# Spread rows in cleared edge records, lists and experts in one block, and a last stage shared by four engines

## What is computed

```python
xn = layernorm(x)
agg = segment_sum(xn[dst] * edge_weight[:, None], src)          # 100000 edges
gnn = relu((xn + agg) @ gW1 + gb1) @ gW2 + gb2                  # 256 -> 512 -> 256
x2  = x + gnn + (heads(xn) + xn)                                # attention without softmax, 8 heads
xn2 = layernorm(x2)
logits = xn2 @ gate_w + gate_b                                  # 16 experts
topk_vals, topk_idx = top_k(logits, 2); w = softmax(topk_vals)
y = xn2 + sum_k w_k * (relu(xn2 @ w1[e_k] + b1[e_k]) @ w2[e_k] + b2[e_k])
out = x2 + layernorm(y) * gamma + beta
```

## Time and profile before

| | |
|---|---|
| median of 3 runs | 2164.53 us (2162.41 to 2166.05) |
| profiled execution | 2162.62 us |
| its span | 2160.9 us |
| granted TensorE clock, mean | 0.884 of full |
| PE busy | 1603.4 us (74%) |
| DVE busy | 1391.8 us (64%) |
| ACT busy | 768.0 us (36%) |
| POOL busy | 1286.3 us (60%) |
| DMA | 231.99 MB, mean 107 GB/s |

### The profile page before, as it was taken

How to read it: one execution, slowest core, us unless ns; L and a number is a source line. 1 busy time by engine, 2 the same in 40 slices (tenths; PEclk the granted TensorE clock), 3 DMA queues, 4 the chain that set the end, 5 groups by cost and what they waited for, 6 DMA issues and landing times. The chain is left out here.

```text
span 2160.9 us, 38464 instructions
## 1 busy us (share of the span) xinstructions
PE 1603.4 (74%) x9490; PEld 1379.4 (64%) x9490; DVE 1391.8 (64%) x4033; ACT 768.0 (36%) x2288; POOL 1286.3 (60%) x1227
## 2 busy tenths in 40 slices
PE   6007888535777778788777877777757999999985
PEld 4006777424555666666666665665546999999964
DVE  5899888548876566666666665566434454545559
ACT  5807898400000233323333232222122333333344
POOL 0005888658877777777777777777602555555420
PEclk9657999767878999999999998999678999999999
DMA  5000110444343444444444444444834652222247
GB/s 168 0 0 20 39 37 21 21 127 137 120 122 108 128 127 129 132 128 128 128 131 132 127 128 120 127 120 128 88 68 147 198 159 71 71 72 70 68 170 278
DMA packets 132685, 231.99 MB, mean 107 GB/s; under 512 B 28678, under 2 KB 85304, under 8 KB 132391
## 3 DMA queue, kind: packets, MB, share of 16 engines
q0 software_dynamic: 56096, 144.39, 24.9%
q1 hardware_dynamic: 48727, 59.76, 9.2%
q10 hardware_dynamic: 27696, 25.83, 3.7%
HBM read 187.46 MB, written 42.43 MB: 106 GB/s over the span
## 5 line engine op out<-in xcount | busy, mean ns | idle before, releaser
L1308 POOL DMA_INDIRECT lower<-xn_rows,lower x858 | 848.0, 988 | 270.5 <-issue 234.6
L1333 PE MATMUL bank<-lower 128*128 x960 | 349.0, 449 | 211.7 <-SPq L1182 176.9
L1333 PEld LDWEIGHTS bank<-lower 128*128 128x128 f32 x960 | 175.3, 214 | 289.0 <-issue 277.7
L1471 DVE TENSOR_TENSOR xh<-xh,bank 128x256 f32 x480 | 199.5, 416 | 245.6 <-PE bank L1334 244.4
L1454 DVE TENSOR_SCALAR lower<-iota_n,lower 128x128 f32<-128x128 f32 x960 | 294.0, 359 | 76.3 <-issue 54.5
L606 POOL DMA_INDIRECT edge_records_sorted<-lower x112 | 202.6, 1809 | 209.0 <-ACT lower L755 179.1
L1334 PE MATMUL bank<-lower 128*128 x960 | 321.7, 420 | 0.0
L683 PE MATMUL bank<-lower 128*64 128x128 f32 x1568 | 190.6, 286 | 113.6 <-ACT lower L739 109.1
L683 PEld LDWEIGHTS bank<-lower 128*64 128x64 f32 x1568 | 184.5, 145 | 117.3 <-DVE lower L941 109.7
L1959 DVE TENSOR_SCALAR arena<-bank,b_tile 128x128 f32<-128x128 f32 x456 | 128.4, 344 | 165.5 <-PE bank L1893 165.5
L1893 PEld LDWEIGHTS bank<-arena 128*128 128x128 f32 x1824 | 224.6, 194 | 13.5 <-issue 7.8
(11 more groups left out here) (330 smaller groups left out, 2348.5 us busy)
## 6 DMA issues: line engine op xcount, KB each, us to landing
lower<-xn_rows,lower POOLq DMA_INDIRECT x858, 2.8
lower<-in_L_ffn_w SPq DMA_DIRECT2D x16, 512.0 KB
upper<-in_L_ffn_w SPq DMA_DIRECT2D x16, 512.0 KB
xn_rows<-xh SPq DMA_DIRECT2D x7, 896.0 KB, 4.2
lower<-xn_rows ACTq DMA_DIRECT2D x49, 128.0 KB
xn_rows<-lower ACTq DMA_DIRECT2D x49, 128.0 KB
x_plus_beta<-lower ACTq DMA_DIRECT2D x49, 128.0 KB
upper<-in_x SPq DMA_DIRECT2D x1, 6144.0 KB
```

The costliest lines, as they stand in the source:

```text
L1308: pool.indirect_dma_start(edge_rows[:, t % ROUND, :], None, xn_dram, bass.IndirectOffsetOnAxis(source.bitcast(U32)[:, t:t + 1], 0)).then_i ...
L1333: pe.matmul(sums_at(u), edge_sel[:, 2 * u % ESEL, :], rows_flat[:, ds(at, D)], start=True, stop=False)
L1471: dve.tensor_tensor(xh[:, at], xh[:, at], sums_at(u), ALU.add).then_inc(s_acc, 1)
```

## The change

Four edits.

- **Cleared records.** GpSimd writes codes into `zeros` before SP copies it out: record j of partition p gets the code (p * 48 + j mod 48) * 128. The weight stays 0. SP's clearing transfer now waits for this. Some semaphores are merged (`buffers_cleared`, `ln1_sums`, the prefix matrix into `buckets`).
- **Marks.** `low_minus` becomes a ring of three (LATE = 3), and the marks of the last three slots are made in the next block, not only that of the last.
- **Lists and experts in one block.** GpSimd's first gathers wait only for `rows_idx`; the mixing weights are made after the lists; the difference of the gates and the experts' numbers are taken after the first of the seven comparisons; SP's loads of expert weights wait for the mixing weights too; ScalarE copies w1 and the transposed rows of the same tile together, w1 first.
- **Last stage.** For the first 16 of the 18 groups ScalarE scales the rows by the reciprocal in place and GpSimd adds x2 + beta, one instruction for a group. VectorE keeps the statistics, the subtraction and the reciprocal; before writing it for group i it waits until ScalarE has scaled group i-2. The last two groups stay with VectorE.

The diff, cut to its core:

```diff
+        FAR = 48
+        LATE = 3
+        low_minus = [carve(TOPK) for _ in range(LATE)]
@@ first block, sync
-                sp.wait_ge(s_zero, 1)
+                sp.wait_ge(s_zero, 2)
                 sp.dma_start(rec_dram[0:ZT * TQ, :].rearrange("(p z) w -> p (z w)", p=P), zeros).then_inc(s_recz, 16)
@@ first block, gpsimd
+                pool.wait_ge(s_zero, 1)
+                pool.iota(zeros.rearrange("p (o i w) -> p o i w", i=FAR, w=REC)[:, :, :, 0], pattern=[[0, ZT // FAR], [P, FAR]], base=0,
+                          channel_multiplier=FAR * P, allow_small_or_imprecise_dtypes=True).then_inc(s_zero, 1)
+
                 pool.wait_ge(s_recz, 16)
@@ second block, scalar
-                    if u - 4 in rank_unit[:-1]:
+                    if u - 4 in rank_unit[:-LATE]:
                         mark(rank_unit.index(u - 4))
@@ lists, sync
+                sp.wait_ge(s_we, 32)
+                sp.sem_inc(s_wready, 1)
+                sp.wait_ge(s_tok[2], 16)
+                sp.wait_ge(s_mixw, 2)
+                for e in range(1, NX):
+                    sp.dma_start(w1_sb[:, e], w1[e].rearrange("(c p) f -> p c f", p=P)).then_inc(s_we, 16)
...
@@ lists, gpsimd
+                pool.wait_ge(s_rows, 2)
+                for t in range(-AHEAD, XT):
+                    if t == 0:
+                        pool.wait_ge(s_rows, 3)
...
@@ lists, scalar
-                last_mark[0](NT - 1, act)
+                for s in range(NT - LATE, NT):
+                    last_mark[0](s, act)
...
+                    t, p, _ = tile_at(j, k + 2)
+                    if is_tile(t):
+                        e = act.value_load(expert_row[0:1, ds(t, 1)], min_val=0, max_val=NX - 1)
+                        if over(t - 1):
+                            act.wait_ge(s_h, t - 1)
+                        act.wait_ge(s_wready, e + 1)
+                        act.activation(w1_tile[p], lower[:, ds(e * (DC * F), DC * F)], ACT.Copy).then_inc(s_w1t, 1)
+                        act.wait_ge(s_tT, t + 1)
+                        act.activation(tokT[p], bank[p][:, 0:D], ACT.Copy).then_inc(s_tTe, 1)
@@ lists, vector
                 for j in range(0, NJ, LCOLS):
+                    if j == LCOLS:
+                        dve.tensor_tensor(gap, tv[:, :, 1], tv[:, :, 0], ALU.subtract).then_inc(s_gap, 1)
+                        dve.wait_ge(s_row, 1)
+                        dve.tensor_copy(expert_row[:], bank[0][0:1, 0:P]).then_inc(s_pick, 1)
+                        dve.tensor_scalar(pick_all[:], bank[0][0:96, 0:P], lane32[:], None, ALU.is_equal).then_inc(s_pick, 1)
@@ last stage
+        SHARED = len(GROUPS) - 2
+        RING = 1
+                def scaled(i):
+                    t0, k0, m = GROUPS[i]
+                    act.wait_ge(s_fcen, t0 + m)
+                    act.wait_ge(s_frs, i + 1)
+                    for k in range(m):
+                        act.activation(first_row(t0 + k), first_row(t0 + k), ACT.Copy, scale=rstd[:, k0 + k:k0 + k + 1]).then_inc(s_fsc, 1)
...
                     act.wait_ge(s_fvar, upto_group(i))
                     act.activation(std[:, k0:k0 + m], mv[:, k0:k0 + m, 1], ACT.Sqrt, bias=eps_col[:]).then_inc(s_fstd, 1)
+                    if 1 <= i <= SHARED:
+                        scaled(i - 1)
...
+                for i, (t0, _, m) in enumerate(GROUPS[:SHARED]):
+                    x2_of = x2_landed(pool, i).rearrange("p (t d) -> p t d", t=m)
+                    rows = pair_rows(t0, m).rearrange("p (t w) -> p t w", t=m)[:, :, 0:D]
+                    pool.wait_ge(s_fsc, t0 + m)
+                    pool.tensor_tensor(rows, rows, x2_of, ALU.add).then_inc(s_fout, m)
...
+                    if i > RING:
+                        dve.wait_ge(s_fsc, upto_group(i - RING - 1))
+                    dve.reciprocal(rstd[:, k0:k0 + m], std[:, k0:k0 + m]).then_inc(s_frs, 1)
+                    if i < SHARED:
+                        return
```

More of the change, by code:

```diff
@@ L282, in gps_layer @@
         zeros = carve(ZT * REC)
+        FAR = 48
+        assert ZT % FAR == 0 and P * FAR <= N and N * P < 1 << 24
         carve = carver(spare, NX * FC * D - NT * D - D)
@@ L1876, in _ @@
             def _(pe):
+                pe.wait_ge(s_wide, 1)
+                pe.matmul(bank[0][:, 0:P], expert_wide, ident[:], start=True, stop=True).then_inc(s_row, 1)
+                pe.wait_ge(s_list, NJ)
+                for j in range(NJ):
+                    if j % LCOLS == 0:
+                        pe.wait_ge(s_high, j // LCOLS + 1)
+                    at = 2 * j * P
+                    pe.matmul(bank[4][:, 0:XT], marks[:, at:at + P], high_hot[:, j, :], start=j == 0, stop=j == NJ - 1)
+                    pe.matmul(bank[5][:, 0:XT], marks[:, at + P:at + 2 * P], high_hot[:, j, :],
+                              start=j == 0, stop=j == NJ - 1).then_inc(s_lists, 1)
+                pe.wait_ge(s_pick, 2)
+                for m in range(FC):
+                    mm = pe.matmul(bank[7][:, m * XT:(m + 1) * XT], bias_split[:, m * P:(m + 1) * P], pick_all[:, 0:XT],
+                                   start=True, stop=True)
+                mm.then_inc(s_b1, 1)
                 expert = {}
@@ new lines, in _ @@
+                dve.tensor_tensor(past_x, iota_pc[:, 0:1].to_broadcast([P, NX - 1]), ends[:, 0:NX - 1],
+                                  ALU.is_ge).then_inc(s_dve, 1)
+                dve.tensor_scalar(high_i, rank_all, 7, None, ALU.arith_shift_right).then_inc(s_dve, 1)
+                dve.wait_ge(s_dve, n.add(3))
+                dve.tensor_reduce(base_of, by_expert(past_base), AX, ALU.add).then_inc(s_dve, 1)
+                dve.tensor_reduce(tile_expert[:], past_x, AX, ALU.add).then_inc(s_dve, 1)
@@ new lines, in _ @@
+                dve.tensor_scalar(plane_i, mark_i, 1, None, ALU.bitwise_and).then_inc(s_dve, 1)
+                dve.wait_ge(s_dve, n.add(2))
+                dve.scalar_tensor_tensor(rows_idx[:], tile_i3, float(P), listed, ALU.mult, ALU.add).then_inc(s_rows, 1)
+                dve.wait_ge(s_rows, 2)
+                dve.scalar_tensor_tensor(dest_all, rows_idx[:], float(TOPK), plane_i, ALU.mult, ALU.add).then_inc(s_dve, 1)
+                dve.wait_ge(s_dve, n.add())
+                dve.tensor_tensor(dest_idx[:], dest_all, spare_at, ALU.max).then_inc(s_rows, 1)
```

229 lines of the change are left out of this document (92 added, 137 removed).

## The result

The changed kernel takes 2146.43 us (2142.93 to 2148.03), the kernel before beside it 2164.74 (2162.41 to 2166.05): ratio 0.9914, 95% interval 0.9897 to 0.9932. That is 18.3 us faster, where 32 were forecast; the time lies 1.4 us above the upper end of the range (2145). The profiled execution took 2146.92 us, its span is 2144.7, against 2160.9 before. On one more chip the ratio was 0.9895 (0.9879 to 0.9912): 2146.24 us, 23.2 fewer than the kernel before there.

What follows compares the result with a forecast made beforehand. GpSimd's gather issue was taken to pace the row fetches, TensorE the experts, VectorE the last stage. 16.8 + 3.6 + 2.1 + 9.4 = 31.9 off 2162.6, plus 1.9 to the median, gave 2132 us, range 2122 to 2145.

Steps and rivals of the forecast that it cites:

- Tail, -16.8: Last 36 row gathers: spreading cleared records' reads over 48 rows issues the last 9.0 us sooner, landing 7.9 faster; 16.8 taken.
- both rivals on the tail: Spread rows stay slow, 2149 us, chance 0.10; or the slot chain binds the tail, 2139 us, chance 0.12.
- the 0.8 to 2.0 of the prediction: Start of the kernel: the added iota takes 0.8 to 2.0 us, and SP's clearing transfer waits that long.
- Marks, -3.6: End of the units' block: moving slots 46 and 47's marks off ScalarE's queue gains 2.4 plus 1.2 us.
- Lists and experts, -2.1: Lists to experts' start: expert gathers and weight loads 2.5 us sooner, third tile 0.4 later; net 2.1 us gained.
- 0.1 behind rows_idx: Lists to experts: with the block's end gone, the first expert gather follows rows_idx in 0.1 us.
- Last stage, -9.4: Final stage: relieving VectorE through ScalarE's scaling and GpSimd's addition ends it at 2151.5 instead of 2160.9 us.
- that rival: Last stage: GpSimd's addition and VectorE exclude each other, 2147 us, or it takes 3.5 ns an element, 2136; chance 0.15 together.
- what is late next is DMA: Last stage: the remaining 16.9 MB at 385 GB/s take 43.9 us, to 2145.9; the last tile adds 5 to 6.
- My walk: Last stage: four engines' orders followed group by group with the assumed durations; before 2161.7, after 2152.3 us.
- SP's stores wait for GpSimd with the DMA share well below 1: Last stage: named as a sign that the prediction would be wrong; no size given.
- The term's side values: Last stage at other rates: -7.1 us at 357 GB/s, -10.6 at 401.

Runs made afterwards that it cites:

- eight blocks: Changed kernel with eight blocks of expert rows under way in the last stage instead of four; 2144.91 us, ratio 0.9877 to the kernel before.

## Why the prediction was wrong

*Tail, -16.8.* Right: -19.2 to the last addition, and 17.5 us of time for the spread alone. (Some 1.5 us of the stretch come back behind it: from the last addition to the first expert gather it is 47.2 us with the spread alone, 45.9 and 45.4 in the kernel before.) The 48 neighbouring rows do not behave like one row, and the slots kept up; both rivals on the tail fell. The iota took 0.94 us, and SP's clearing transfer left 1.47 us later (6.73 instead of 5.26), within the 0.8 to 2.0 of the prediction. That it cost nothing agrees with the first row gather: 462.6 without the iota (the changed kernel without the spread), 460.9 and 463.4 with it.

*Marks, -3.6.* Right in place and size (3.3 by the four rows above; -4.2 in the stretch).

*Lists and experts, -2.1.* Measured -1.2. The step that failed is the gather "0.1 behind rows_idx": it came 0.8 behind (1624.57 to 1625.39). The cause stays open. By the program the gather waits only for rows_idx. Its row names the instruction of dest_idx (L1925), which raises the same semaphore. In all profiles of kernels with this block the gather starts 0.82 us after rows_idx ends and 0.2 after dest_idx ends, so the traces can't tell the two apart.

*Last stage, -9.4.* Measured -4.0. The durations held: three L2118 in 1.24 us, GpSimd 2.36 us for 1024 elements or 2.3 ns each (2.2 taken), ScalarE's scaling 0.43 (0.40 taken). So GpSimd neither excluded VectorE nor was slow, and that rival fell. By the Trainium skill (GPSIMD Engine Reference, Performance versus the Vector engine) an addition of 2048 elements takes 4497 ns, 2.2 each: the trace agrees. By the Trainium skill (SBUF — State Buffer, Who interferes with whom) a VectorE instruction with at most one input in SBUF, outside its two-port modes, doesn't contend with GpSimd. The trace agrees: four L2118 take 1.63 us from 2101.28 on, inside GpSimd's addition of 2101.13 to 2102.95.

What failed is the step "what is late next is DMA", with the remaining bytes at 385 GB/s. The transfers could do it (391 to 401 with eight blocks), but in the changed kernel they moved 272 to 338 GB/s from 2086 to 2110. The next load stood on SP behind a store, which now waits for a chain of VectorE, ScalarE and GpSimd instead of VectorE alone. My walk had the four compute engines' orders and a rate for the DMA, not SP's order. The prediction had named this sign ("SP's stores wait for GpSimd with the DMA share well below 1") and given it no price. By the table it is 2.9 to 3.8 us, by the two whole stages 4.1, and with the latter the term would have been 4.0 + 4.1 = 8.1 against 9.4.

Even with eight blocks ScalarE is as full as the transfers, 23.2 of the 24 us from 2100 to 2124 beside 401 GB/s, so DMA alone is not shown to be the bound there either. The term's side values don't follow from its plain sum: 16.9 MB at 357 GB/s give -6.0 and not -7.1, at 401 -11.2 and not -10.6.

*A cost that no term had:* with GpSimd's addition in the program the calm fetches took 5.2 us longer. The prediction costed the addition where it runs. This cancels the 4 to 5 us that the last stage won.

*The profile.* 4.5 us of the ledger are a favourable execution of the kernel before, and its calm fetches (1064.2) are the shortest of five as well; I had carried its 1.9 us below the median, and no more. What the tail gave above its term, 2.4 us, makes the miss smaller; nothing in the prediction earned that. The sum with the missing cost and the two terms that failed, 31.9 - 5.2 - (9.4 - 4.0) - (2.1 - 1.2) = 20.4, lies between the 18.3 and 23.2 us of the two comparisons.

## What to carry to other kernels

When work moves from one engine to two, follow the store that waits for it into its queue, and look what is issued behind it: here loads freed from that place were worth some 3 us, where the whole move was worth 4 to 5. When a stage's length varies in its start, compare a stretch inside it. Before adding an operation of a new kind to the engine that paces another stage, put one dummy of it at the program's end and look at that stage's median duration. And where a padded index makes all lanes read one row, spread the padding over real rows; here it cost one iota.

## What the hardware showed unexpectedly

128 lanes reading one row hold the DMA share at 0.98 with 74 to 78 GB/s. Reading 48 rows, two or three lanes each, is as fast as reading the rows of real edges (0.41 and 126 GB/s against 0.42 and 121). The row gathers on GpSimd took 946 ns (median, minimum 940 or 942) in the old program, 953 or 957 with a tensor_tensor in it that runs after all of them, 957 with a tensor_copy, and 949 with iotas for memsets. And the same kernel takes 2165 us on one chip and 2412 on another, where the mean granted clock was 0.84 instead of 0.88. In the kernels profiled there the fetches waited for freed buffers instead of for GpSimd; what makes those chips so much slower stays open.
